# Maxima over partitions by two float32 products instead of GpSimd's all-reduce, the FFN scales placed earlier, and layer 0 waiting per channel half

## The chip, the cores and the metric

The kernel runs on one core of one Trainium2 chip. The metric is the device time of one execution in microseconds. A core has five engines with queues of their own, each worked through in order: PE (TensorE, the matrix engine), DVE (VectorE), ACT (ScalarE), POOL (GpSimd) and SP (SyncE, which issues the DMAs here). They meet only at semaphores.

## What is computed

The reference is a block with attention and a feed-forward part side by side, both fed by the same layer norm. x has 16 batches of 512 tokens and 256 channels; there are 8 heads of width 128.

```python
xn = layernorm(x)                                   # over the 256 channels
q, k, v = xn @ wq, xn @ wk, xn @ wv                 # per head; q and k rotated by position (rope)
p = softmax(q @ k.T / 128 - 1e30 * (i < j))         # causal
attn = sum over heads of (p @ v) @ wo
h = s0 * concat(xn, -xn) @ sign(k0)                 # sign: +1 where the boolean is true, else -1
h = 2 * relu(h)
h = 2 * relu(s1 * h @ sign(k1))                     # 1024 -> 1024
out = x + attn + s2 * h @ sign(k2)                  # 1024 -> 256
```

All of it is float32. k0 is 512 x 1024, k1 1024 x 1024, k2 1024 x 256, and s0, s1, s2 are scalars.

## The kernel before

**Numbers.** Every float32 operand of a product is held as two half-precision parts, high and low, and a product is taken as two or three half-precision products that add up in PSUM. The weights wq, wk, wv and wo are first divided by a power of two that is worked out on the chip from the largest absolute value in each: `largest` (L254) reduces one weight along the free axis to a column per partition on VectorE; `powers` (L259) brings two such columns together over the 128 partitions with GpSimd's partition_all_reduce, cuts them to a power of two and takes its reciprocal; `split_w` (L274) writes the high part on ScalarE and the low part on VectorE. powers(0) serves wq and wk, powers(2) serves wv and wo.

**Order.** The program is written out for all 16 x 8 = 128 heads by a planner. `Fill` (L356) takes the next of 8 PSUM banks in a ring and waits for those who read it last; its products go to TensorE's queue at once, and each adds its columns/512 to a clock (L369). What the other engines do with the result is put off with `at(delay, job)` (L343) and put down by `run_due` (L347) when the clock has come that far, or earlier when `need` (L351) asks for it. So the order of each queue is fixed when the program is written.

**Before the heads.** SyncE issues the loads of x, the scales, k0, k1, wq, wk, the tables cos and sin, k2, wv, later wo. `norm`, `norm_apply` and `first_T` normalise batch 0 and turn it by float32 transposes to xT (channels on partitions, two channel halves c = 0, 1, each with a high part from ScalarE and a low part from VectorE). `subtract_k0` and `sign_k0` build W0, `convert_k1` (GpSimd and ScalarE) W1, `convert_k2` (GpSimd) W2. `ffn_scales` (L293) works out signs and factors; `convert_k1` waits for some of them. Then `layer0(0, n)` for n = 0..7 (L632) and `layer1(0, 0)`, `powers(0)`, the first quarter of wq and wk, `layer1(0, 1)`.

**Heads.** The loop over slots g = -2..129 (L796) puts down qk(g + 2, w) for w = 0 (q) and 1 (k), scores(g + 1), values(g - 1), and between them fillers (layer0, layer1, layer2, v_proj, proj) in three groups. qk (L458) has six steps of each of its two fills: ScalarE swaps the halves (L478, L479, tile tb), VectorE multiplies by cos (straight, L485, tile ta), GpSimd multiplies tb by sin and adds (crossed, L489 and L491), ScalarE takes the high part (L497), VectorE the low part (L501). scores (L508) waits for the low parts of q and k of its head. In slot -2 this stands after the two fills of qk(0): the second quarter of wq and wk, `convert_k2`, `largest` of wv and wo, `powers(2)`, both halves of wv, and `pads` (GpSimd zeroes eight strips); layer1(0, 2) and layer1(0, 3) come behind, and layer1(0, 4) is in slot -1 ahead of scores(0). `straight`, `swap` of k and `crossed` of head 0 fall due only within layer1(0, 2).

The code as it was, with the line numbers of the profile:

Of the kernel before, what the change touches and what calls it, by code (L numbers as in the profile page):

```python
# [83 lines left out]
def block_kernel(nc, x, wq, wk, wv, wo, k0, k1, k2, s3, cosT, sinT, out):  # L84
    ctx = ExitStack()
    with ctx:
        def sb(name, shape, dt=F32):
            return ctx.enter_context(nc.sbuf_tensor(name, shape, dt))
# [33 lines left out]
        RI = sb("ri", [128, 4, 4])  # L122
        RK = sb("rk", [128, 4, 4])
        S3 = sb("s3", [128, 3])
        AM = sb("am", [128, 4])
        AR = sb("ar", [128, 4])
        P2 = sb("p2", [128, 4])
        KN = sb("kn", [128, 4])
        SG = sb("sg", [128, 8])
        SC = sb("sc", [128, 8])  # L130
        BANK = [ctx.enter_context(nc.psum_tensor(f"bank{i}", [128, 512], F32)) for i in range(8)]


# [68 lines left out]

        c = pool.put(lambda e: e.memset(ID[:], 0.0))
        m = pool.put(lambda e: e.memset(MASK[:], 0.0))
        done["half"] = pool.put(lambda e: e.memset(HALF[:], -0.5))
        pool.wait(c)
        done["ident"] = pool.put(lambda e: e.affine_select(
# [44 lines left out]


        def largest(i, n):  # L254
            dve.wait(done["w_in", n])
            done["largest", i] = dve.put(lambda e: e.tensor_reduce(AM[:, i:i + 1], stage3[n], AX.XY, ALU.max,  # L256
                                                                   apply_absolute_value=True))

        def powers(i, least):  # L259

            pool.wait(done["largest", i], done["largest", i + 1])
            a = pool.put(lambda e: e.partition_all_reduce(AR[:, i:i + 2], AM[:, i:i + 2], 128,
                                                          bass.bass_isa.ReduceOp.max))
            dve.wait(a)
            a = dve.put(lambda e: e.tensor_scalar(AR[:, i:i + 2], AR[:, i:i + 2], least, None, ALU.max))
            dve.wait(a)
            a = dve.put(lambda e: e.tensor_scalar(P2[:, i:i + 2].bitcast(I32), AR[:, i:i + 2].bitcast(I32),
                                                  0x7F800000, None, ALU.bitwise_and))
            dve.wait(a)
            a = dve.put(lambda e: e.tensor_scalar(P2[:, i:i + 2], P2[:, i:i + 2], 2.0 ** -6, None, ALU.mult))  # L270
            dve.wait(a)
            done["KN", i] = dve.put(lambda e: e.reciprocal(KN[:, i:i + 2], P2[:, i:i + 2]))

# [12 lines left out]
        def signs():  # L286

            dve.wait(done["s3"])
            a = dve.put(lambda e: e.tensor_scalar(SG[:, 0:3], S3[:], 0.0, None, ALU.is_ge))
            dve.wait(a)  # L290
            done["signs"] = dve.put(lambda e: e.tensor_scalar(SG[:, 0:3], SG[:, 0:3], 2.0, -1.0, ALU.mult, ALU.add))

        def ffn_scales():  # L293

            dve.wait(done["signs"])
            dve.put(lambda e: e.tensor_scalar(SG[:, 3:4], SG[:, 1:2], 2.0 ** -8, None, ALU.mult))
            dve.put(lambda e: e.tensor_scalar(SG[:, 4:5], SG[:, 1:2], -2.0 ** -9, None, ALU.mult))
            a = dve.put(lambda e: e.tensor_tensor(SC[:, 2:4], S3[:, 0:2], SG[:, 0:2], ALU.mult))
            done["k1_signs"] = a
            dve.wait(a)  # L300
            a = dve.put(lambda e: e.tensor_scalar(SC[:, 4:5], SC[:, 2:3], SC[:, 3:4], 64.0, ALU.mult, ALU.mult))
            dve.wait(a)
            done["ffn_scale"] = dve.put(lambda e: e.tensor_scalar(SC[:, 5:6], SC[:, 4:5], S3[:, 2:3], None, ALU.mult))

# [3 lines left out]
        def subtract_k0(half):  # L308

            dve.wait(done["k_in", 0])  # L310
            done["k0_diff", half] = dve.put(lambda e: e.tensor_tensor(
                W0[:, :, half * 512:half * 512 + 512], halves(K0S[:, 0:2048], half), halves(K0S[:, 2048:4096], half),
                ALU.subtract))
# [37 lines left out]
        def need(key):  # L351
            while key not in done:
                later.pop(0)[1]()
            return done[key]
# [275 lines left out]
                  ("vp", b, grp, t, HI), ("vp", b, grp, t, LO), scale=2.0 ** -6, free=free)  # L630

        def layer0(b, n):  # L632
            pe.wait(done["W0", n // 4], need(("xT", b, 0)), need(("xT", b, 1)))
            f = Fill(("l0", b, n))
            f.group((0, 512), [(W0[:, c, n * 128:n * 128 + 128], XT[:, b % 2, s, :, c, :])
                               for c in range(2) for s in (HI, LO)])
            f.end([("h0", b, n, LO)])
            free = [("l1", b - 1, 7)] if b else []
            split(f, H0[:, HI, n, :], H0[:, LO, n, :], ("h0", b, n, HI), ("h0", b, n, LO), relu=True, free=free)
# [125 lines left out]
        act.put(lambda e: e.activation(MV[:, 1, 0, 0:1], HALF[:, 0:1], ACT.Copy))  # L765
        norm(0)
        signs()
        subtract_k0(0)
        sign_k0(0)
        norm_apply(0)  # L770
        subtract_k0(1)
        last_load()
        ffn_scales()
        first_T()
        while later:
            later.pop(0)[1]()
# [6 lines left out]
        for n in range(8):  # L783
            layer0(0, n)
            run_due()
        layer1(0, 0)
        run_due()
        powers(0, 2.0 ** -10)
# [7 lines left out]
        for g in range(-2, G + 2):  # L796
            jobs = [job for _, job in sorted(fillers.get(g, []), key=lambda item: item[0])]
            third = [jobs[k * len(jobs) // 3:(k + 1) * len(jobs) // 3] for k in range(3)]
            if g + 2 < G:
                for w in range(2):  # L800
                    qk(g + 2, w)
                    run_due()
            if g == -2:
                split_w("q", 0, 1, 4)
                split_w("k", 1, 1, 4)
                convert_k2()
                largest(2, "v")
                largest(3, "o")
                powers(2, 2.0 ** -30)
                for p in range(2):  # L810
                    split_w("v", 2, p, 2)
                pads()
            if g == -1:
                for p in (2, 3):
                    split_w("q", 0, p, 4)
                    split_w("k", 1, p, 4)
            if g == 2:
                for p in range(2):
                    split_w("o", 3, p, 2)
                done["attn_scale"] = dve.put(lambda e: e.tensor_scalar(SC[:, 6:7], P2[:, 2:3], P2[:, 3:4], None,  # L820
                                                                       ALU.mult))
            for job in third[0]:
                job()
                run_due()
            if 0 <= g + 1 < G:
                scores(g + 1)
                run_due()
            for job in third[1]:
                job()
                run_due()  # L830
            if 0 <= g - 1 < G:
                values(g - 1)
                run_due()
            for job in third[2]:
                job()
                run_due()
            if g == -1:
                normal(1)
            if g > 3 and g % 8 == 3 and g // 8 + 1 < NB:
                normal(g // 8 + 1)  # L840
# [56 lines left out]
```

How the kernel before makes its waits and increments, by code:

```python
    def wait(self, *events):  # L61
        for sem, value in events:
            if self.seen.get(id(sem), 0) < value:
                self.seen[id(sem)] = value
                self.items.append(lambda e, s=sem, v=value: e.wait_ge(s, v))
# [1 line left out]
    def put(self, make, signal=True):  # L67
        if not signal:
            self.items.append(make)
            return None
        self.count += 1
        self.items.append(lambda e: make(e).then_inc(self.sem, 1))
        return (self.sem, self.count)
# [1 line left out]
    def dma(self, make, sem, value):  # L75
        self.items.append(lambda e: make(e).then_inc(sem, 16))
        return (sem, value)
```

## Time and profile before

| | |
|---|---|
| three runs | 1819.17, 1819.51 and 1821.78 us, median 1819.51 |
| profiled execution | 1822.18 us, its span 1820.1 us |
| mean granted TensorE clock | 0.988 |
| busy share | TensorE 97%, VectorE 79%, ScalarE 60%, GpSimd 57% |
| TensorE by 40ths of the span, in tenths | 7, 5, 8, 9, 9, 7, then 9 throughout |

The span runs from the first to the last instruction; the time of an execution is a little more. Each engine's busy time counts instructions of that engine only; TensorE's ends are modelled. A timeline row stands for one instruction or for several alike, with the idle time before it and what ended that.

### The profile page before, as it was taken

The page shows a single profiled execution, that of the slowest core. Times are in us where ns is not written, and L with a number is a line of the kernel's source. Part 1 is how long each engine was busy: PE and PEld are TensorE (multiplying, and loading weights), DVE is VectorE, ACT ScalarE, POOL GpSimd, SP SyncE. Part 2 cuts the span into 40 slices and gives each one's busy share as a digit, 9 for nine tenths or more (in the row PEclk, how much of TensorE's full clock was granted, in tenths as well). Part 3 has the DMA queues.
Part 4 walks back from the last instruction along what each step waited for, and adds up shares of the span by engine and source line. Part 5 has one row for each costly group of instructions (what it writes and reads, how often), then busy time and mean ns, then how long its engine had stood idle before and what let it go on. Part 6 is the DMA issues. An engine that isn't in the chain of part 4 may idle for free.

```text
span 1820.1 us, 30382 instructions
## 1 busy us (share of the span) xinstructions
PE 1763.6 (97%) x11272; PEld 1058.5 (58%) x11272; DVE 1441.9 (79%) x3271; ACT 1092.6 (60%) x2340; POOL 1043.6 (57%) x1065
## 2 busy tenths in 40 slices
PE   7589979999999999999999999999999999999999
PEld 3255646566565666656566565566656566565566
DVE  6689878887878878788887878878797887878865
ACT  4466555665665656566665665656566665665653
POOL 2467655565655555565565655556565565655552
PEclk9899989999999999999999999999999999999999
DMA  4033524343433333442344444334433444334333
GB/s 168 18 64 70 93 47 74 83 71 76 70 71 81 68 79 64 81 78 56 84 71 76 69 72 82 66 77 67 78 80 54 86 70 76 67 73 82 64 70 65
DMA packets 454820, 133.84 MB, mean 74 GB/s; under 512 B 434704, under 2 KB 453648, under 8 KB 454672
## 3 DMA queue, kind: packets, MB, share of 16 engines
q1 hardware_dynamic: 454672, 131.90, 38.1%
q8 instruction: 89, 1.46, 0.3%
q14 instruction: 59, 0.48, 0.1%
HBM read 14.94 MB, written 8.39 MB: 13 GB/s over the span
## 4 chain that ended last, share of the span: by engine, by line
PE 89%; DVE 6%; ACT 3%; issue 1%; POOL 1%; DMA 0%; SPq 0%; DVEq 0%; POOLq 0%
PE bank L368 89%; DVE ph L566 1%; ACT p L543 1%; DVE p L529 1%; DVE ta L485 1%; POOL ta L491 0%; DVE h L410 0%; DVE v L413 0%; DVE qk L501 0%; DMA o<-in_k 0%; DVE am L256 0%; POOL tb L489 0%; ACT tb L479 0%; DVE nm L537 0%; ACT tb L478 0%
## 5 line engine op out<-in xcount | busy, mean ns | idle before, releaser
L560 POOL TENSOR_SCALAR ph<-p,ri 128x512 f16<-128x512 f32 (+3 forms) x512 | 340.4, 665 | 312.4 <-DVE rk L550 277.6
L489 POOL TENSOR_TENSOR tb<-tb,sin 128x512 f32<-128x512 f32 x256 | 329.1, 1286 | 310.1 <-ACT tb L479 299.7
L368 PE MATMUL bank<-h,w 128*128 128x512 f16 x2048 | 462.4, 379 | 0.0
L491 POOL TENSOR_TENSOR ta<-ta,tb 128x512 f32<-128x512 f32 x256 | 344.7, 1347 | 71.7 <-DVE ta L485 55.5
L543 ACT ACTIVATE p<-p,nm,sc 128x512 f32<-128x512 f32 (+3 forms) x512 | 327.3, 641 | 39.9 <-DVE nm L537 39.9
L368 PEld LDWEIGHTS bank<-h,w 128*128 128x128 f16 x2048 | 199.0, 98 | 217.9
L478 ACT ACTIVATE tb<-bank 64x512 f32<-64x512 f32 x256 | 152.1, 594 | 286.2 <-PE bank L368 275.6
L566 DVE SCALAR_TENSOR_TENSOR ph<-p,rk,ph 128x512 f16<-128x512 f32 (+3 forms) x512 | 306.1, 638 | 3.5 <-POOL ph L560 3.5
L497 ACT ACTIVATE qk<-ta 128x512 f16<-128x512 f32 x256 | 160.1, 625 | 189.8 <-POOL ta L491 189.7
L368 PE MATMUL bank<-qk 128*128 128x512 f16 (+3 forms) x1536 | 234.1, 303 | 31.7 <-DVE qk L501 31.7
L485 DVE TENSOR_TENSOR ta<-bank,cos 128x512 f32<-128x512 f32 x256 | 175.4, 686 | 90.8 <-ACT tb L479 90.3
L529 DVE CUSTOM_DVE_ANT_0 p<-bank,mask 128x512 f32<-128x512 f32 (+3 forms) x512 | 226.4, 485 | 23.9 <-PE bank L368 23.3
L368 PE MATMUL bank<-pt,v 128*128 128x256 f16 (+1 forms) x2304 | 232.7, 256 | 2.5 <-DVE ta L485 1.6
L368 PEld LDWEIGHTS bank<-pt,v 128*128 128x128 f16 x2304 | 204.5, 98 | 49.3 <-issue 2.4
L501 DVE TENSOR_TENSOR qk<-ta,qk 128x512 f16<-128x512 f32 x256 | 215.7, 842 | 13.4 <-ACT qk L497 12.3
L368 PEld LDWEIGHTS bank<-qk 128*128 128x128 f16 x1536 | 135.1, 99 | 137.7 <-DVE qk L501 35.1
L405 ACT ACTIVATE h<-bank 128x512 f16<-128x512 f32 x256 | 148.6, 587 | 71.6 <-PE bank L368 70.1
L368 PE MATMUL bank<-xT,wq 128*128 128x512 f16 x768 | 186.7, 379 | 1.6 <-DVE h L410 1.6
L368 PE MATMUL bank<-xT,wk 128*128 128x512 f16 x768 | 186.6, 379 | 0.0
L368 PE MATMUL bank<-wv,xT 128*128 128x512 f16 x768 | 181.6, 379 | 2.2 <-DVE ta L485 2.2
L410 DVE SCALAR_TENSOR_TENSOR h<-bank,h 128x512 f16<-128x512 f32 x256 | 172.4, 684 | 8.9 <-ACT h L405 1.4
L368 PE MATMUL bank<-wo,o 128*128 128x256 f16 x1536 | 172.9, 273 | 0.0
(75 smaller groups left out, 1714.5 us busy)
## 6 DMA issues: line engine op xcount, KB each, us to landing
out<-xnat SPq DMA_DIRECT2D x32, 256.0 KB, 2.4
xnat<-in_x SPq DMA_DIRECT2D x15, 512.0 KB, 4.0
pt<-ph SPq DMA_TRANSPOSE x256, 4.3
o<-in_k SPq DMA_DIRECT2D x1, 1024.0 KB, 7.9
v<-in_wq SPq DMA_DIRECT2D x1, 1024.0 KB, 9.9
v<-in_wk SPq DMA_DIRECT2D x1, 1024.0 KB, 11.5
ph<-in_wv SPq DMA_DIRECT2D x1, 1024.0 KB, 13.4
o<-in_wo SPq DMA_DIRECT2D x1, 1024.0 KB, 10.8
```

Of the source, the lines that this page charges most:

```text
L368: self.todo.append(lambda e: e.matmul(self.ps[:, cols[0]:cols[1]], lhsT, rhs, start=start, stop=stop))
L410: done[lo_key] = dve.put(lambda e: e.scalar_tensor_tensor(lo_out, src, 0.0, hi_out, ALU.max, ALU.subtract))
L478: act.put(lambda e: e.activation(TB[0:64, r, :], f.ps[64:128, :], ACT.Copy))
L485: done["rot_a", n] = dve.put(lambda e: e.tensor_tensor(ta, f.ps[:, :], COS[:], ALU.mult))
L489: a = pool.put(lambda e: e.tensor_tensor(tb, tb, SIN[:], ALU.mult))
L491: done["rot", n] = pool.put(lambda e: e.tensor_tensor(ta, ta, tb, ALU.add))
L497: done["qk_hi", n] = act.put(lambda e: e.activation(hi, ta, ACT.Copy))
L501: done["qk_lo", n] = dve.put(lambda e: e.tensor_tensor(lo, ta, hi, ALU.subtract))
L529: done["max", g, i] = dve.put(lambda e, i=i, a=a, w=w: e.tensor_tensor_reduce(out=P[:, r, S_OFF[i]:S_OFF[i] + w], in0=f.ps[:, a:a + w], in ...
L543: done["exp", g, i] = act.put(lambda e: e.activation(v, v, ACT.Exp, bias=NM[:, g % 4, i:i + 1], scale=SC[:, 0:1], accum_out=SM[:, g % 4, i ...
L560: done["P_hi", g, i] = pool.put(lambda e: e.tensor_scalar(part(r, i, HI), v, RI[:, g % 4, i:i + 1], 4096.0, ALU.mult, ALU.mult))
L566: done["P_lo", g, i] = dve.put(lambda e: e.scalar_tensor_tensor(part(r, i, LO), v, RK[:, g % 4, i:i + 1], part(r, i, HI), ALU.mult, ALU.su ...
```

## The change

`powers` loses its GpSimd instruction. `largest` now writes its column into a 128-column strip of zeros (AM, float32, in the memory that xT of batch 1 uses later), one strip for each pair of weights, the pair in columns 0 and 1. `turn_largest` multiplies the strip by the identity on TensorE, so that row 0 and row 1 of a bank hold the maxima of the two weights, and VectorE reduces the 128 columns of the bank to one. `powers` cuts these to powers of two on VectorE, puts them on the diagonal of two columns (DG), and a second product with a matrix of ones (ONES) brings both numbers to all partitions; VectorE copies them from the bank and takes reciprocals. GpSimd zeroes AM and sets ONES at the start. turn_largest(0) stands ahead of layer1(0, 0); turn_largest(2) stands between layer1(0, 2) and layer1(0, 3), and powers(2), the split of wv and the pads stand behind layer1(0, 3).

`ffn_scales` moves from behind the second `subtract_k0` to ahead of the first. `layer0` waits for channel half 0 of xT before its first two products and for half 1 before its last two.

```diff
-        AM = sb("am", [128, 4])
+        DG = sb("dg", [128, 4])
...
+        AM = XT[:, 1].rearrange("p s t c n -> p (s t c n)").bitcast(F32)[:, 0:256].rearrange("p (i n) -> p i n", i=2)
+        ONES = XT[:, 1].rearrange("p s t c n -> p (s t c n)").bitcast(F32)[:, 256:384]
...
+        done["am_zero"] = pool.put(lambda e: e.memset(AM, 0.0))
+        done["ones"] = pool.put(lambda e: e.memset(ONES, 1.0))
...
         def largest(i, n):
-            dve.wait(done["w_in", n])
-            done["largest", i] = dve.put(lambda e: e.tensor_reduce(AM[:, i:i + 1], stage3[n], AX.XY, ALU.max,
+            dve.wait(done["w_in", n], done["am_zero"])
+            done["largest", i] = dve.put(lambda e: e.tensor_reduce(AM[:, i // 2, i % 2:i % 2 + 1], stage3[n], AX.XY, ALU.max,
                                                                    apply_absolute_value=True))
+        def turn_largest(i):
+            pe.wait(done["largest", i], done["largest", i + 1], done["am_zero"], done["ident"])
+            f = Fill(("am", i))
+            f.mm((0, 128), AM[:, i // 2], ID[:], True, True)
+            f.end([("am_max", i)])
+            dve.wait(done[f.key])
+            done["am_max", i] = dve.put(lambda e: e.tensor_reduce(AR[:, i:i + 1], f.ps[:, 0:128], AX.X, ALU.max))
         def powers(i, least):
-            pool.wait(done["largest", i], done["largest", i + 1])
-            a = pool.put(lambda e: e.partition_all_reduce(AR[:, i:i + 2], AM[:, i:i + 2], 128,
-                                                          bass.bass_isa.ReduceOp.max))
+            dve.wait(done["am_max", i])
+            a = dve.put(lambda e: e.tensor_scalar(AR[:, i:i + 1], AR[:, i:i + 1], least, None, ALU.max))
             dve.wait(a)
...
+            a = dve.put(lambda e: e.tensor_scalar(AR[:, i + 1:i + 2].bitcast(I32), AR[:, i:i + 1].bitcast(I32),
                                                   0x7F800000, None, ALU.bitwise_and))
             dve.wait(a)
-            a = dve.put(lambda e: e.tensor_scalar(P2[:, i:i + 2], P2[:, i:i + 2], 2.0 ** -6, None, ALU.mult))
+            a = dve.put(lambda e: e.tensor_scalar(DG[:, i:i + 2], ID[:, 0:2], AR[:, i + 1:i + 2], 2.0 ** -6,
+                                                  ALU.mult, ALU.mult))
+            pe.wait(a, done["ones"])
+            f = Fill(("p2", i))
+            f.mm((0, 2), ONES, DG[:, i:i + 2], True, True)
+            f.end([("KN", i)])
+            dve.wait(done[f.key])
+            a = dve.put(lambda e: e.tensor_scalar(P2[:, i:i + 2], f.ps[:, 0:2], 1.0, None, ALU.mult))
             dve.wait(a)
             done["KN", i] = dve.put(lambda e: e.reciprocal(KN[:, i:i + 2], P2[:, i:i + 2]))
...
         def layer0(b, n):
-            pe.wait(done["W0", n // 4], need(("xT", b, 0)), need(("xT", b, 1)))
+            pe.wait(done["W0", n // 4])
             f = Fill(("l0", b, n))
-            f.group((0, 512), [(W0[:, c, n * 128:n * 128 + 128], XT[:, b % 2, s, :, c, :])
-                               for c in range(2) for s in (HI, LO)])
+            for c in range(2):
+                f.wait(need(("xT", b, c)))
+                for s in (HI, LO):
+                    f.mm((0, 512), W0[:, c, n * 128:n * 128 + 128], XT[:, b % 2, s, :, c, :], c + s == 0, c + s == 2)
...
         signs()
+        ffn_scales()
         subtract_k0(0)
...
         last_load()
-        ffn_scales()
...
+        turn_largest(0)
         layer1(0, 0)
...
                 largest(3, "o")
-                powers(2, 2.0 ** -30)
-                for p in range(2):
-                    split_w("v", 2, p, 2)
-                pads()
...
+            if g == -2:
+                turn_largest(2)
             for job in third[2]:
                 job()
                 run_due()
+            if g == -2:
+                powers(2, 2.0 ** -30)
+                for p in range(2):
+                    split_w("v", 2, p, 2)
+                pads()
```

## Rows read from the trace of the kernel before

**Rows 1.** Waits of TensorE, whole span: total us, times, longest us.

```profile
PE bank L368 <- DVE qk L501: 31.7, 7, 17.2
```

**Rows 2.** Timeline of TensorE: start us, us, what, xcount, idle before.

```profile
28.87 1.46 PE L368 MATMUL bank<-xT,wq 128*128 128x512 f16 x6
...
31.46 7.07 PE L368 MATMUL bank<-h,w 128*128 128x512 f16 x32
...
40.95 3.62 PE L368 MATMUL bank<-h,w 128*128 128x512 f16 x16
61.75 3.18 PE L368 MATMUL bank<-qk 128*128 128x512 f16 x12 [17.18 <-DVE qk L501]
...
77.71 1.79 PE L368 MATMUL bank<-qk 128*128 128x512 f16 x12
```

**Rows 3.** Windows: length, busy us (x count) by engine, granted clock, DMA share, GB/s.

```profile
60.00:62.00 2.00, 0.25 (x1) 0.14 (x2) 0.98 (x2) 1.70 (x3) 0.22 (x1) 0.50 0.00 0
80.00:100.00 20.00, 16.05 (x104) 9.46 (x103) 19.89 (x44) 13.43 (x30) 13.30 (x13) 1.00 0.35 66
300.00:600.00 300.00, 300.00 (x1927) 179.81 (x1925) 241.59 (x555) 183.02 (x392) 177.09 (x179) 1.00 0.39 75
```

**Rows 4.** Timeline of VectorE from 35 to 66 us, as rows 2.

```profile
35.88 2.27 DVE L256 TENSOR_REDUCE am<-o 128x1 f32<-128x2048 f32 x1
...
43.84 2.48 DVE L283 SCALAR_TENSOR_TENSOR wv<-ph,kn,wv 128x1024 f16<-128x1024 f32 x2 [1.22 <-ACT wv L281]
...
60.91 0.69 DVE L501 TENSOR_TENSOR qk<-ta,qk 128x512 f16<-128x512 f32 x1 [0.62 <-ACT qk L497]
62.89 1.11 DVE L283 SCALAR_TENSOR_TENSOR wq<-v,kn,wq 128x512 f16<-128x512 f32 x1 [1.29 <-ACT wq L281]
...
65.92 1.28 DVE L485 TENSOR_TENSOR ta<-bank,cos 128x512 f32<-128x512 f32 x2
```

**Rows 5.** Timeline of ScalarE from 30 to 58 us, as rows 2.

```profile
30.98 0.59 ACT L479 ACTIVATE tb<-bank 64x512 f32<-64x512 f32 x1
...
42.66 2.19 ACT L281 ACTIVATE wv<-ph,kn 128x1024 f16<-128x1024 f32 x2 [9.73 <-DVE kn L272]
...
57.36 0.63 ACT L497 ACTIVATE qk<-ta 128x512 f16<-128x512 f32 x1 [11.28 <-POOL ta L491]
```

**Rows 6.** Timeline of GpSimd from 11 to 56 us, the same columns.

```profile
11.71 5.91 POOL L326 TENSOR_SCALAR w<-o,sg 128x1024 f16<-128x1024 uint8 x5 [4.88 <-DVE sc L298]
24.86 0.37 POOL L262 PARTITION_ALL_REDUCE ar<-am  x1 [7.24 <-issue]
33.10 2.43 POOL L334 TENSOR_SCALAR w<-o 128x2048 f16<-128x2048 uint8 x1 [7.86 <-issue]
41.44 0.37 POOL L262 PARTITION_ALL_REDUCE ar<-am  x1 [5.92 <-issue]
46.44 1.23 POOL L223 MEMSET ph<- 128x128 f16 x8 [4.62 <-DVE wv L283]
54.73 1.26 POOL L489 TENSOR_TENSOR tb<-tb,sin 128x512 f32<-128x512 f32 x1 [7.06 <-issue]
```

**Rows 7.** Timeline of all engines at the start, as rows 2.

```profile
7.68 1.23 DVE L311 TENSOR_TENSOR w<-o 128x1024 f16<-128x1024 uint8 x1 [1.66 <-DMA o<-in_k]
...
11.14 1.08 ACT L405 ACTIVATE xT<-bank 128x512 f16<-128x512 f32 x2 [1.05 <-PE bank L372]
...
11.81 0.21 DVE L303 TENSOR_SCALAR sc<-sc,s 128x1 f32<-128x1 f32 x1
11.94 1.28 DVE L413 SCALAR_TENSOR_TENSOR xT<-bank,xT 128x512 f16<-128x512 f32 x2
...
13.36 8.76 PE L368 MATMUL bank<-xT,w 128*128 128x512 f16 x32 [2.05 <-ACT w L319]
```

**Rows 8.** Groups by line and form: busy us, mean ns, idle before.

```profile
L529 DVE CUSTOM_DVE_ANT_0 p<-bank,mask 128x128 f32<-128x128 f32 x128 | 36.4, 285 | 0.0
L372 PE MATMUL bank<-ident,xp 128*128 128x128 f32 x8 | 1.9, 424 | 9.4 <-DVE xp L250 9.4
```

More of the change, by code:

```diff
@@ L259, in powers @@
         def powers(i, least):
-            pool.wait(done["largest", i], done["largest", i + 1])
-            a = pool.put(lambda e: e.partition_all_reduce(AR[:, i:i + 2], AM[:, i:i + 2], 128,
-                                                          bass.bass_isa.ReduceOp.max))
+            dve.wait(done["am_max", i])
+            a = dve.put(lambda e: e.tensor_scalar(AR[:, i:i + 1], AR[:, i:i + 1], least, None, ALU.max))
             dve.wait(a)
-            a = dve.put(lambda e: e.tensor_scalar(AR[:, i:i + 2], AR[:, i:i + 2], least, None, ALU.max))
@@ L266, in powers @@
-            dve.wait(a)
-            a = dve.put(lambda e: e.tensor_scalar(P2[:, i:i + 2].bitcast(I32), AR[:, i:i + 2].bitcast(I32),
+            a = dve.put(lambda e: e.tensor_scalar(AR[:, i + 1:i + 2].bitcast(I32), AR[:, i:i + 1].bitcast(I32),
                                                   0x7F800000, None, ALU.bitwise_and))
             dve.wait(a)
-            a = dve.put(lambda e: e.tensor_scalar(P2[:, i:i + 2], P2[:, i:i + 2], 2.0 ** -6, None, ALU.mult))
+            a = dve.put(lambda e: e.tensor_scalar(DG[:, i:i + 2], ID[:, 0:2], AR[:, i + 1:i + 2], 2.0 ** -6,
+                                                  ALU.mult, ALU.mult))
```

## The prediction

> **What bounds the kernel now.** I read four views, in this order. First the waits of TensorE [rows 1]: it stands 31.7 us in seven waits for line 501, and one of the seven is 17.2 us; the other six come to 14.5 us, 2.4 us each. Then its timeline [rows 2]: layer1(0, 4) begins at 40.95 and ends at 44.57, and the next product, scores(0), begins at 61.75. That hole is the largest thing in the span that is not work. From 300 us on TensorE is busy in 300.00 of 300 us at full clock [rows 3], so whatever the first 62 us give back, the rest should pass on whole.
>
> Then the hole is followed back. scores(0) waits for the low part of the rotated k of head 0, VectorE's line 501 at 60.91 [rows 4], which waits for line 497 on ScalarE, and that had waited 11.28 us for GpSimd [rows 5]. GpSimd's own timeline [rows 6] shows the reason: its first rotation product (tb, line 489) begins at 54.73 after 7.06 us idle that end on "issue", which means that nothing the profile sees was missing. Its operand, the swapped halves, was written by 31.57 (30.98 + 0.59) [rows 5]. Before that the same timeline has three more such holes: 7.24 us before the first all-reduce over partitions, 7.86 us before k2's conversion behind it, 5.92 us before the second all-reduce. I read this as 6 to 8 us for every change from ordinary work to the all-reduce or back; the five conversions at 11.71, which waited for VectorE alone, show no such hole. The second reason is order: straight(0), swap(1) and crossed(0) were put down behind powers(2), the split of wv and the pads, so line 485 for head 0 could run only after the split of wv (43.84 + 2.48 = 46.32) [rows 4], and tb only after the pads (46.44 + 1.23 = 47.67) [rows 6].
>
> Here the Trainium skill speaks against the change: GPSIMD Engine Reference, section 4.1 (Engine selection), gives reductions along the partition dimension to GpSimd. The all-reduce itself is indeed shown with 0.37 us [rows 6], less than any replacement; the four holes, 28.1 us together, are not in that figure. Section 2.1 (Instruction dispatch) of the same page has a first call to a freshly loaded kernel pay about 6 us with no instruction shown, 5.95 us in its measurement. The trace agrees with the size (5.92 to 7.86) but shows it four times for one kind of kernel, on the way back too. With 5.95 in place of 7.06 for the last hole the removed time would be 1.1 us less; my sum does not go by either, since it is built from the new order below.
>
> **The change part by part.**
>
> *FFN scales ahead of k0.* VectorE is idle 1.66 us before 7.68, until k0 lands; five operations of 0.14 to 0.21 us [rows 7] fit there: cost nothing (0.8 us if k0 came earlier). They leave the place before 11.94, where they stood until 12.02 in front of the low parts of xT. ScalarE has the first high part done at about 11.7 (11.14, two in 1.08), so the first low part runs 11.75 to 12.4 in place of 11.94 to 12.6, the second ends near 13.0. GpSimd's conversion of k1 may start up to 1.4 us earlier than 11.71; layer 1 needs it near 22 and it ended at 17.6, so nothing.
>
> *Layer 0 waits per channel half.* Its first product starts after channel 0's low part, at 12.5 in place of 13.36 [rows 7]; the two products of channel 0 (8.76/32 = 0.27 each) last about until channel 1 is there. Gain 0.8 us, between 0 and 0.9. All of it is in front of weights that come later, so by itself it moves little.
>
> *powers(0).* TensorE gets a 128x128 float32 product after layer 0 and a two-column one after layer1(0, 0). The trace has no plain float32 product. The nearest row is the float32 transpose, 0.424 us each [rows 8]; a half-precision product of as many columns is 3.62/16/4 = 0.06 us [rows 2]. Ends: 0.06 and 0.85 (twice the transpose); I take 0.42 and 0.25. On VectorE a reduction of 128 columns of PSUM comes in: nearest row 0.285 us [rows 8], ends 0.2 and 0.6, taken 0.3. It stands in VectorE's queue ahead of three low parts of layer 0 and waits for TensorE to finish layer 0 at 21.3 and the product at 21.7; the three then end at 24.0 (3 x 0.64), and layer1(0, 0), which began at 21.7, needs the last of them at 24.8. No stall. The maxima over q and k come ahead of all low parts of layer 0 in VectorE's queue, so they are ready. Then three small operations, the second product at 25.2, two small ones: the reciprocal stands near 25.9, and before it stood at 26.05 (25.23, where the all-reduce ended, and four operations of 0.2 at most [rows 7]). So wq and wk split as before, and the 0.8 us won at layer 0 is spent on the two products: qk(0) begins at 28.8 +- 0.5, as before (28.87) [rows 2].
>
> *The second turn, and what moved.* layer1(0, 2) runs 31.46 to 35.0 as before. Behind it on TensorE now stands turn_largest(2), which waits for VectorE's maximum over wo: 35.88 + 2.28 = 38.15 [rows 4]. This is the added wait: TensorE stands 3.2 us, layer1(0, 3) is queued behind it. Product 38.2 to 38.6, layer1(0, 3) to 42.1. Meanwhile the rotation of head 0 is no longer behind wv. VectorE: straight(0) 38.15 to 38.8, straight(1) to 39.4, the reduction to 39.7. GpSimd has no hole left, and tb is done at 32.8, 1.26 after the swap (k2's conversion can follow k1's, ended at 17.6, since the row names nothing that it waited for); ta 38.85 to 40.1 (1.26) [rows 6]. ScalarE 40.15 to 40.8 (0.63) [rows 5], VectorE's low part to 41.4 (0.69), a low part of layer 1 to 42.1 (0.64), three small ones to 42.7. Second product 42.7 to 42.95 (TensorE stands another 0.6), copy and reciprocal to 43.4. ScalarE splits wv to 45.6 (2.19), then turns to the high part of k of head 0, to 46.3. VectorE: wv 44.6 to 47.05, a low part of layer 1 to 47.7, line 501 for k to 48.35. TensorE: qk(1) 42.95 to 45.6 (31.46 - 28.87 = 2.6), layer1(0, 4) to 49.2. So scores(0) begins at 49.2, bound by TensorE's own work by 0.8 us: 12.55 us before 61.75.
>
> *Behind scores(0).* Before, its twelve products took 3.18 us, since the granted clock stood at 0.50 at the hole's end [rows 3], the 1.2 GHz level; at 77.71 the same twelve took 1.79 [rows 2]. With TensorE busy from 42.7 on, 1.4 us more are won: 13.95 at scores(1). The other engines' chain runs from line 501 for k (60.91 before, 47.7 new) through four splits to straight(2). Before, 65.92 - 60.91 = 5.0, of which 1.29 was a wait for ScalarE's split of wq [rows 4]; ScalarE now is ahead of VectorE: 3.7, so straight(2) at 51.4, 14.5 us earlier. In 80 to 100 us VectorE is busy 19.89 of 20 and TensorE only 16.05 [rows 3]: that stretch follows VectorE's chain, so its 14.5 counts more than TensorE's 13.95. I take 14.3. The wv split and pads end near 48.3 and are wanted only by what follows scores(0): nothing. The two new strips that GpSimd fills at the start (AM, ONES) stand in its first 3 us, before anything needs them: nothing (0.5 us if they were late).
>
> Sum: 0 (start) + 12.55 (the hole's 17.2, less 3.8 of new standing and 0.7 for the two later products, to rounding) + 1.75 (1.4 of clock, and 0.35 of VectorE's lead where TensorE follows it) = 14.3 us. The profiled execution took 1822.18 around a span of 1820.10; the runs' median is 1819.51, 2.7 below it. The gain is a difference inside the span, so it comes off the median: 1805.2.
>
> **Rivals.**
>
> *The clock falls in the new wait* (chance 0.20). TensorE stands 3.2 us at turn_largest(2); if its clock drops to 0.50 as after the hole, layer1(0, 3) loses 1.4 us and the second product comes 0.8 later. For it: a stop costs the clock here already [rows 3]. Against: 3.2 is far from 17.2. scores(0) at 50.6, the rest 0.7 late: gain 13.0, 1806.5.
>
> *GpSimd's holes stay* (0.08): they belong to first uses of code, not to the all-reduce. For it: "issue" names no cause. Against: line 334's operation ran five times as line 326 before its hole. Then k2's conversion ends as late as 35.5, tb after a hole of 7.06 at 43.9, ta 45.1, and by the same steps scores(0) comes near 54 with a fallen clock: gain 7 to 9, 1811.
>
> *Given back later* (0.04): the six other waits, 14.5 us, hang on something that does not move, and grow by what is won. Against: no load is in the chains there, each wait is for line 501. 1819, within 0.2% (3.6 us, about what a measurement can tell).
>
> *Slower by a shifted order* (0.03). The four new fills add 1.0 to the planner's clock and four places to the bank ring; jobs go down by that clock. If a tie flips so that once in a batch scores waits as it does in the six other waits, 2.4 us, 15 batches cost 36: 1841. It decides from six such waits (14.3/2.4). Against: all due times are relative to the same clock, and the steady stretch has no slack to show [rows 3].
>
> *More than forecast* (0.03): with VectorE ahead, waits between 80 and 100 (3.95 us of TensorE's 20) shrink too: 1802.
>
> **Numbers.** My forecast holds 0.62, with 1803.5 to 1807 of its own. The range 1801 to 1811 takes in the fallen clock, the larger gain, twice the float32 price on both products in the path, and the edge of the staying holes. Faster: 0.62 + 0.20 + 0.08 + 0.03 = 0.93; within 0.2% 0.04; slower 0.03.
>
> **What would show it.** No holes on "issue" in GpSimd's timeline; tb of head 0 in the thirties; TensorE idle 3 us near 35 with VectorE's line 256 as its end, and under 1 us near 42; scores(0) at 49 and quick; the wait list's 17.2 gone. Wrong if a hole stands before line 489, if a wait for line 501 over 4 us remains before 60, or if TensorE is not full after 300.

## The result and the profile after

Beside four runs of the kernel before (median 1820.06 us) the changed kernel took 1807.28 us (four runs, 1804.13 to 1809.90): ratio 0.9928, 95% interval 0.9910 to 0.9946, so 12.8 us less by the medians. Timed again later on one chip with others (e9 below) it took 1807.09 against 1818.63, ratio 0.9931 (0.9917 to 0.9946). Forecast were 1805.2 us, a gain of 14.3, in a range of 1801 to 1811. The two profiled executions of the table are at the slow end of their kernels' runs. Below, "after" is the profile of the changed kernel.

| us | before | after |
|---|---|---|
| profiled execution, its span | 1822.18, 1820.1 | 1809.90, 1808.0 |
| TensorE busy in the span | 1763.6 | 1765.8 |
| longest wait of TensorE for the rotation's low part | 17.2 | 7.5 |
| scores(0) begins | 61.75 | 50.82 |
| straight(2), head 1's first rotation product on VectorE, begins | 65.92 | 53.80 |

In the changed file the lines lie lower: products L385 (L368 before), tb and ta on GpSimd L506 and L508 (L489, L491), straight on VectorE L502 (L485), the rotation's low part L518 (L501), `split_w` on VectorE L300 (L283), `largest` L260 (its column AM lies in xT's memory, so rows call it xT).

TensorE's waits after (total us, times, longest), to be held against [rows 1]:

```profile
PE bank L385 <- DVE qk L518: 14.4, 6, 7.5
...
PE bank L385 <- DVE xT L260: 3.6, 1, 3.6
```

The 17.2 is gone and the six others are left, 14.4 us as against 14.5, the longest 7.5. The new entry is the wait of turn_largest(2) for the maximum of wo. TensorE's timeline after, against [rows 2]:

```profile
12.68 9.90 PE L385 MATMUL bank<-xT,w 128*128 128x512 f16 x32 [1.29 <-DVE xT L430]
22.42 0.39 PE L385 MATMUL bank<-ident,xT 128*128 128x128 f32 x2
22.64 3.62 PE L385 MATMUL bank<-h,w 128*128 128x512 f16 x16
26.09 0.28 PE L385 MATMUL bank<-dg,xT 128*128 128x2 f32 x2
...
29.68 1.46 PE L385 MATMUL bank<-xT,wq 128*128 128x512 f16 x6
...
39.48 0.76 PE L385 MATMUL bank<-ident,xT 128*128 128x128 f32 x2 [3.60 <-DVE xT L260]
40.04 4.76 PE L385 MATMUL bank<-h,w 128*128 128x512 f16 x16
44.63 0.28 PE L385 MATMUL bank<-dg,xT 128*128 128x2 f32 x2
...
50.82 1.79 PE L385 MATMUL bank<-qk 128*128 128x512 f16 x12
...
65.39 1.79 PE L385 MATMUL bank<-qk 128*128 128x512 f16 x12
```

A float32 product shows as two instructions. The one of 128 columns holds the next product up by 0.22 us (22.42 to 22.64), the one of two columns by 0.14. layer1(0, 3) at 40.04 takes 4.76 where such a fill takes 3.62. The windows say why (columns as in [rows 3]):

```profile
36.00:38.00 2.00, 0.00 (x0) 0.00 (x0) 2.00 (x2) 0.00 (x0) 0.00 (x0) 1.00 0.00 0
38.00:39.00 1.00, 0.00 (x0) 0.00 (x0) 1.00 (x1) 0.00 (x0) 0.00 (x0) 0.96 0.00 0
39.00:40.00 1.00, 0.52 (x2) 0.53 (x3) 1.00 (x3) 0.00 (x0) 0.00 (x0) 0.50 0.00 0
...
42.00:44.00 2.00, 2.00 (x10) 0.85 (x9) 1.89 (x4) 0.49 (x2) 1.92 (x2) 0.91 0.00 0
```

TensorE did nothing from 35.9, and its granted clock fell to 0.50, the 1.2 GHz level, near 39 and was back at full within 42 to 44. GpSimd after, against [rows 6]:

```profile
18.54 1.90 POOL L351 TENSOR_SCALAR w<-o 128x2048 f16<-128x2048 uint8 x1 [1.37 <-DMA o<-in_k]
32.47 1.27 POOL L506 TENSOR_TENSOR tb<-tb,sin 128x512 f32<-128x512 f32 x1 [12.03 <-ACT tb L496]
40.08 1.26 POOL L508 TENSOR_TENSOR ta<-ta,tb 128x512 f32<-128x512 f32 x1 [6.34 <-DVE ta L502]
```

From 11 us on no hole ends on "issue" any more: k2's conversion waits for its load, tb for its swap, ta for VectorE. VectorE after, against [rows 4]:

```profile
33.16 1.12 DVE L300 SCALAR_TENSOR_TENSOR wq<-v,kn,wq 128x512 f16<-128x512 f32 x1 [1.96 <-ACT wq L298]
...
37.07 2.27 DVE L260 TENSOR_REDUCE xT<-o 128x1 f32<-128x2048 f32 x1
39.26 1.27 DVE L502 TENSOR_TENSOR ta<-bank,cos 128x512 f32<-128x512 f32 x2
...
42.04 1.08 DVE L518 TENSOR_TENSOR qk<-ta,qk 128x512 f16<-128x512 f32 x1 [1.31 <-ACT qk L514]
...
49.53 0.68 DVE L518 TENSOR_TENSOR qk<-ta,qk 128x512 f16<-128x512 f32 x1
50.12 0.75 DVE L300 SCALAR_TENSOR_TENSOR wq<-v,kn,wq 128x512 f16<-128x512 f32 x1
50.79 1.77 DVE L300 SCALAR_TENSOR_TENSOR wk<-v,kn,wk 128x512 f16<-128x512 f32 x1
...
53.80 1.27 DVE L502 TENSOR_TENSOR ta<-bank,cos 128x512 f32<-128x512 f32 x2
```

The low part of head 0's k (L518 at 49.53) now ends before TensorE comes to scores(0), but straight(2) stands 4.27 us behind it, since one of four like splits took 1.77 in place of 0.75.

### The profile page after: what moved, and what is told of

It is laid out like the page before. It is cut to its first block, busy times and chain, and to the rows that moved or that the text cites. A ratio compares the mean times of both kernels' runs of the same rounds, so it can differ in the third digit from the quotient of the medians.

```text
span 1808.0 us, 30390 instructions
## 1 busy us (share of the span) xinstructions
PE 1765.8 (98%) x11280; PEld 1058.0 (59%) x11280; DVE 1448.0 (80%) x3275; ACT 1092.7 (60%) x2340; POOL 1041.2 (58%) x1065
## 4 chain that ended last, share of the span: by engine, by line
PE 90%; DVE 6%; ACT 3%; POOL 1%; DMA 0%; issue 0%; SPq 0%; DVEq 0%; POOLq 0%
PE bank L385 90%; DVE ph L583 1%; ACT p L560 1%; DVE p L546 1%; DVE ta L502 1%; DVE h L427 0%; DVE qk L518 0%; DVE v L430 0%; DMA o<-in_k 0%; POOL ta L508 0%; DVE xT L260 0%; DVE nm L554 0%; ACT tb L496 0%; ACT tb L495 0%; DVE wo L300 0%
## 5 line engine op out<-in xcount | busy, mean ns | idle before, releaser
L506 POOL TENSOR_TENSOR tb<-tb,sin 128x512 f32<-128x512 f32 x256 | 328.9, 1285 | 311.8 <-ACT tb L496 308.4
L385 PE MATMUL bank<-h,w 128*128 128x512 f16 x2048 | 463.9, 380 | 0.0
L508 POOL TENSOR_TENSOR ta<-ta,tb 128x512 f32<-128x512 f32 x256 | 344.8, 1347 | 77.7 <-DVE ta L502 61.6
L385 PEld LDWEIGHTS bank<-h,w 128*128 128x128 f16 x2048 | 199.1, 98 | 218.4 <-issue 1.5
L502 DVE TENSOR_TENSOR ta<-bank,cos 128x512 f32<-128x512 f32 x256 | 175.4, 686 | 90.4 <-ACT tb L496 90.4
L385 PE MATMUL bank<-qk 128*128 128x512 f16 (+3 forms) x1536 | 232.7, 302 | 14.4 <-DVE qk L518 14.4
L385 PE MATMUL bank<-pt,v 128*128 128x256 f16 (+1 forms) x2304 | 232.9, 256 | 2.5 <-DVE ta L502 1.6
L385 PEld LDWEIGHTS bank<-pt,v 128*128 128x128 f16 x2304 | 204.1, 98 | 49.8 <-issue 2.4
L518 DVE TENSOR_TENSOR qk<-ta,qk 128x512 f16<-128x512 f32 x256 | 214.5, 838 | 3.3 <-ACT qk L514 2.5
L385 PEld LDWEIGHTS bank<-qk 128*128 128x128 f16 x1536 | 134.6, 98 | 119.5 <-DVE qk L518 17.4
L385 PE MATMUL bank<-xT,wq 128*128 128x512 f16 x768 | 186.7, 379 | 1.6 <-DVE h L427 1.6
L385 PE MATMUL bank<-xT,wk 128*128 128x512 f16 x768 | 186.7, 379 | 0.0
L385 PE MATMUL bank<-wv,xT 128*128 128x512 f16 x768 | 181.6, 379 | 2.4 <-DVE ta L502 2.4
L385 PE MATMUL bank<-wo,o 128*128 128x256 f16 x1536 | 172.9, 273 | 0.0
## 6 DMA issues: line engine op xcount, KB each, us to landing
o<-in_wo SPq DMA_DIRECT2D x1, 1024.0 KB, 10.7
```

The costliest lines, as they stand in the source:

```text
L385: self.todo.append(lambda e: e.matmul(self.ps[:, cols[0]:cols[1]], lhsT, rhs, start=start, stop=stop))
L502: done["rot_a", n] = dve.put(lambda e: e.tensor_tensor(ta, f.ps[:, :], COS[:], ALU.mult))
L506: a = pool.put(lambda e: e.tensor_tensor(tb, tb, SIN[:], ALU.mult))
L508: done["rot", n] = pool.put(lambda e: e.tensor_tensor(ta, ta, tb, ALU.add))
L518: done["qk_lo", n] = dve.put(lambda e: e.tensor_tensor(lo, ta, hi, ALU.subtract))
```

## The experiments

My theory: the gain has two parts, GpSimd's holes at each change to and from the all-reduce, and the order that lets head 0's rotation go ahead of wv. The rivals: only the holes count; only the order counts.

**e1: the order without the products.** The whole change, but `powers` as before:

```diff
 # before, with the two start edits, and in slot -2:
-    powers(2, ...); split_w("v", ...) x2; pads()     # behind largest(3, "o")
+    powers(2, ...); split_w("v", ...) x2; pads()     # behind layer1(0, 3)
```

> The whole change but for the products: GpSimd's all-reduce stays, and powers(2), the split of wv and the pads stand behind layer1(0, 3). My theory (holes and order each hold a part): four holes of 6 to 8 us on GpSimd remain, but tb and ta of head 0 run ahead of the third; the third and the fourth now delay wv's split and tb of head 1; scores(0) near 55, straight(2) near 59, ta of head 1 near 64 (66.74 before), gain over the kernel before 2 to 5 us. Rival 'only the order counts': gain 12 as in the whole change. Rival 'only the holes count': gain 0.

Measured: 1818.93 against 1819.40 us, ratio 1.0001 (0.9991 to 1.0010): nothing, at most 1.6 us. GpSimd's timeline:

```profile
34.70 1.69 POOL L489 TENSOR_TENSOR tb<-tb,sin 128x512 f32<-128x512 f32 x1
...
50.28 0.37 POOL L262 PARTITION_ALL_REDUCE ar<-am  x1 [5.72 <-issue]
55.28 1.23 POOL L223 MEMSET ph<- 128x128 f16 x8 [4.63 <-DVE wv L283]
63.55 1.26 POOL L489 TENSOR_TENSOR tb<-tb,sin 128x512 f32<-128x512 f32 x1 [7.04 <-issue]
```

tb of head 0 did move ahead (54.73 before), and scores(0) began at 56.51, 5.2 us earlier. But the two holes only moved behind it: the last now stands in front of tb of head 1, whose ta follows at 64.89 as against 66.74 before. I had expected 2 to 5 us; of the 5.2 not even 2 can be seen in the time. scores(0) was not the place to measure, and straight(2), 7.0 us earlier (58.92), was not either, since the last hole stands behind both; ta of head 1 was, only 1.85 us earlier.

**e2: the products without the order.** turn_largest(2), powers(2), the split of wv and the pads directly behind `largest(3, "o")`:

```diff
 # on the changed kernel, which has these lines around layer1(0, 3)
                 largest(3, "o")
+                turn_largest(2)
+                powers(2, 2.0 ** -30); split_w("v", 2, p, 2) x2; pads()
```

> The products in place of the all-reduce, but turn_largest(2), powers(2), the split of wv and the pads directly behind the maxima of wv and wo as before the change. My theory: no holes on GpSimd; TensorE stands some 7 us behind qk(0) until the maximum of wo (39), layer 1 runs behind it with a fallen clock; scores(0) near 55, gain over the kernel before 6 to 9 us. Rival 'only the holes count': gain 12. Rival 'only the order counts': gain 0 to 2.

Measured: 1810.75 against 1819.40, ratio 0.9954 (0.9941 to 0.9967): 6.0 to 10.7 us less, as expected. TensorE:

```profile
37.46 0.76 PE L385 MATMUL bank<-ident,xT 128*128 128x128 f32 x2 [6.68 <-DVE xT L260]
39.24 0.59 PE L385 MATMUL bank<-dg,xT 128*128 128x2 f32 x2 [1.02 <-DVE dg L280]
39.70 8.85 PE L385 MATMUL bank<-h,w 128*128 128x512 f16 x32
...
54.42 1.79 PE L385 MATMUL bank<-qk 128*128 128x512 f16 x12
```

By the medians the products alone are worth 8.6 us, the order alone 0.5, both together 11.5 to 12.8: the new order pays 3 to 4 us, and only once the holes are gone. The intervals of e2 and of the whole change overlap, and against e3, timed beside e2, the medians differ by 1.9 us only; the traces show the part more clearly, with straight(2) 47.9 us behind the first transpose in e2 (56.47, 8.55) and 44.4 in the changed kernel (53.80, 9.45). "Only the order counts" falls by both runs. "Only the holes count" fits e1 (0) and falls by e2, where its 12 us lie outside the interval and a part is left for the order.

**e3 and e4: the two start edits left out, and alone.**

```diff
 # e3, on the changed kernel; e4 has the reverse on the kernel before
-        ffn_scales()                 # ahead of subtract_k0(0)
+        ffn_scales()                 # behind last_load()
-            for c in range(2): f.wait(need(("xT", b, c))) ...
+            pe.wait(done["W0", n // 4], need(("xT", b, 0)), need(("xT", b, 1))); f.group(...)
```

> The change without the two edits of the start (FFN scales back behind the second subtract_k0, layer 0 waits for both channel halves). My theory: what layer 0 wins comes in front of weights that come later, so the time is that of the whole change within 1 us (1806 to 1809); layer 0 begins near 13.4 in place of 12.7. Rival 'the start passes on': 0.7 to 0.9 us slower than the whole change.

> The kernel before with the two edits of the start alone. My theory: layer 0 begins near 12.6 in place of 13.36, the hole of 17 us before scores(0) stays as it hangs on GpSimd; gain 0 to 0.9 us, which can't be told from nothing. Rival: 1 us or more.

Measured: e3 1808.83, ratio to before 0.9942 (0.9928 to 0.9955), which overlaps the changed kernel's 0.9931 and can't be told from it; e4 1818.52, ratio 0.9996 (0.9988 to 1.0005), nothing. The moment at which k0 lands differs between executions (the first transposes begin between 8.4 and 9.9), so starts are read from there: layer 0 begins 3.23 us behind the first transpose with the edits (after, e1, e2, e4 and others alike) and 3.98 without. But its 32 products take 8.35 to 10.02 us with the edits, in most traces over 9.1, and 8.54 to 8.76 without; the products at the start stand 0.43 us apart, twice the later spacing, though the granted clock reads 1.00 there, and that stretch is mostly longer where layer 0 starts earlier; why is not shown. So in most traces what is won at its start is gone at its end (not in e4 and e12).

**e5: two all-reduces that nobody reads**, in the changed kernel:

```diff
                 convert_k2()
+                for i in range(2):   # IDLE is a new tile
+                    pool.put(lambda e, i=i: e.partition_all_reduce(IDLE[:, 2*i:2*i+2], HALF[:, 2*i:2*i+2], 128, ReduceOp.max))
```

> The changed kernel with two all-reduces over partitions behind k2's conversion that nobody reads. My theory (a hole stands at each change between ordinary work and the all-reduce): 6 to 8 us idle on 'issue' before the first, under 0.5 us before the second, 6 to 8 us before tb of head 0 (line 489 of the kernel before). GpSimd would reach tb near 35 to 36 in place of 32.5, and ta is held by VectorE until 40 anyway, so the time stays within 2 us of the changed kernel. Rival 'each all-reduce takes its 6 to 8 us': a hole before both, none before tb. Rival 'first use of code': a hole before the first, none before the second and none before tb.

GpSimd, and the swap that writes tb on ScalarE:

```profile
17.79 1.90 POOL L352 TENSOR_SCALAR w<-o 128x2048 f16<-128x2048 uint8 x1 [1.54 <-DMA o<-in_k]
25.82 0.72 POOL L829 PARTITION_ALL_REDUCE idle<-half  x2 [6.13 <-issue]
33.97 1.26 POOL L507 TENSOR_TENSOR tb<-tb,sin 128x512 f32<-128x512 f32 x1 [7.43 <-ACT tb L497]
```
```profile
30.37 0.59 ACT L497 ACTIVATE tb<-bank 64x512 f32<-64x512 f32 x1
```

One hole of 6.13 before the first, none between the two, 7.43 from their end to tb. The profile puts the last down to the swap, but that had ended at 30.96, 3.0 us before. So a hole belongs to each change, in and out, as the theory has it. "Each all-reduce takes its time" (two holes in, none out) falls. "First use of code" falls by e1 above: tb's first run there stands directly behind k2's conversion (34.70), and 7.04 us stand before a later one. (In the changed kernel tb came behind a wait of 12.03 us, which could have hidden a hole.) Two things go with this. The eight memsets behind the second all-reduce began without a hole on "issue", and the 7.06 us came behind them [rows 6]. And of the 5.92 us before that all-reduce only 3.3 held anything up, since the maximum of wo ended at 38.15 [rows 4]. The one time, 1809.17, is within the changed kernel's runs.

**e6 and e11: TensorE kept busy in the new wait.** Sixteen products that nobody reads ahead of turn_largest(2); in e11 they don't count on the planner's clock:

```diff
+                now = clock[0]                                   # e11
+                for i in range(4):
+                    f = Fill(("warm", i))
+                    for n in range(4):
+                        f.mm((0, 512), W0[:, 0, 0:128], XT[:, 0, HI, :, 0, :], n == 0, n == 3)
+                    f.end([])
+                clock[0] = now                                   # e11
                 turn_largest(2)
```

> The changed kernel with sixteen products that nobody reads (3.5 us) ahead of turn_largest(2), where TensorE stood 3.60 us and its clock fell to 0.50. If the fallen clock has a price of its own: granted clock 1.00 from 34 to 46, layer1(0, 3) takes 3.6 in place of 4.76, scores(0) 0.5 to 1.1 us earlier (near 50), straight(2) up to 0.9 us earlier. If VectorE's chain sets both anyway: layer1(0, 3) 3.6, scores(0) and straight(2) unchanged within 0.3.

> As e6, sixteen products that nobody reads ahead of turn_largest(2), but they don't count on the planner's clock, so that every queue keeps the changed kernel's order. My theory: granted clock 1.00 throughout, layer1(0, 3) 3.6 us, TensorE stands 0.9 us at the second product, straight(2) 14.3 us behind the end of the maximum of wo (14.5 in the changed kernel's profile, 16.2 in e5): the wait itself costs VectorE's chain nothing, its fallen clock 0 to 1.9 us. Rival 'the extra products cost': more than 15.

e6 did not keep the order and settles nothing: its sixteen units on the planner's clock brought line 518 of k ahead of powers(2) on VectorE, the second product waited 2.58 us for that, and scores(0) was 51.33. The clock did stay at 1.00. e11 keeps the order; TensorE and VectorE:

```profile
39.36 3.63 PE L385 MATMUL bank<-h,w 128*128 128x512 f16 x16
43.69 0.38 PE L385 MATMUL bank<-dg,xT 128*128 128x2 f32 x2 [0.71 <-DVE dg L280]
```
```profile
38.63 1.27 DVE L502 TENSOR_TENSOR ta<-bank,cos 128x512 f32<-128x512 f32 x2
...
52.96 1.27 DVE L502 TENSOR_TENSOR ta<-bank,cos 128x512 f32<-128x512 f32 x2
```

TensorE in e3, where the clock did not fall in a wait of the same length:

```profile
37.82 0.46 PE L385 MATMUL bank<-ident,xT 128*128 128x128 f32 x2 [3.60 <-DVE xT L260]
38.12 3.62 PE L385 MATMUL bank<-h,w 128*128 128x512 f16 x16
```

From straight(0) to straight(2) VectorE's chain takes 14.33 us in e11. In the changed kernel's profile it takes 14.54 (layer1(0, 3) 4.76 us), in e3 14.33 (3.62), in e5 16.17 (6.38, the clock at 0.50 until past 42). So the wait costs this chain nothing, since VectorE itself is what TensorE waits for; its fallen clock costs 0.2 us in one execution and 1.8 in another, and nothing where it does not fall. e11's one time, 1809.79, shows no gain from it.

**e12: tb of head 1 held behind VectorE's four splits.**

```diff
                 pool.wait(done["swap", n], done["sin"])
+                if n == 2: pool.wait(done["W", "k", 3])
```

> The changed kernel, but GpSimd's tb of head 1's q (the one that ran beside VectorE's four splits of wq and wk) waits until the last of the four is done. In the changed kernel one of the four took 1.77 us and the others 0.74, and tb 1.68 where it takes 1.27 alone. Theory 'the two engines stand in each other's way when VectorE reads two operands from SBUF': all four splits take 0.74 to 0.75, tb 1.27, straight(2) begins 1.0 us earlier behind line 501 of head 0's k (3.2 to 3.3 in place of 4.27), ta of head 1's q ends 0.3 to 0.7 us earlier although tb starts 2 us later. Rival 'the long split has another cause': 1.77 stays, and ta of head 1 ends 1 us later.

VectorE, then GpSimd:

```profile
47.26 0.68 DVE L520 TENSOR_TENSOR qk<-ta,qk 128x512 f16<-128x512 f32 x1
47.86 0.75 DVE L300 SCALAR_TENSOR_TENSOR wq<-v,kn,wq 128x512 f16<-128x512 f32 x1
48.52 0.75 DVE L300 SCALAR_TENSOR_TENSOR wk<-v,kn,wk 128x512 f16<-128x512 f32 x1
...
50.51 1.29 DVE L502 TENSOR_TENSOR ta<-bank,cos 128x512 f32<-128x512 f32 x2
```
```profile
50.74 1.27 POOL L508 TENSOR_TENSOR tb<-tb,sin 128x512 f32<-128x512 f32 x1 [2.65 <-DVE wk L300]
52.09 1.27 POOL L510 TENSOR_TENSOR ta<-ta,tb 128x512 f32<-128x512 f32 x1
```

All four splits take 0.75, tb 1.27 in place of 1.68, and straight(2) stands 3.25 us behind the low part in place of 4.27. ta of head 1 ends 6.10 us behind it (6.36 in the changed kernel), though tb waited 2.65. The one time, 1805.41, lies within the changed kernel's runs and shows no gain by itself.

**e7, e8 and e10: a better order.** e7 (and e10, the same kernel timed beside e9) splits the second quarter of wq and wk a slot later, so that VectorE has the maxima of wv and wo earlier; e8 also moves the last two quarters:

```diff
-                split_w("q", 0, 1, 4); split_w("k", 1, 1, 4)     # slot -2, ahead of the maxima
-            if g == -1:  for p in (2, 3): ...
+            if g == -1:  for p in (1, 2, 3): split_w("q", 0, p, 4); split_w("k", 1, p, 4)     # e7
+            # e8: p = 1 in slot -1, p = 2 and 3 in slot 0
```

> The changed kernel with the second quarter of wq and wk split a slot later, so that VectorE takes the maxima of wv and wo 3.5 us earlier. My theory: the added wait goes: the maximum of wo ends near 36, TensorE stands under 0.5 us at turn_largest(2) and up to 1.3 at the second product, clock 1.00, scores(0) at 46 to 48 (50.8), straight(2) at 50 to 51.5 (53.8), the whole 2 to 4 us less than the changed kernel (1803 to 1805). Rival 'given back later': the waits from 62 to 120 grow by what is won, time as the changed kernel.

> As e7, and the third and fourth quarters of wq and wk are split behind qk(2) in place of behind qk(1). My theory: VectorE's chain from line 501 of head 0's k to straight(2) holds two splits in place of six: straight(2) 2 to 3 us earlier than in e7 (47.5 to 49). The four splits then fall where VectorE is busier: 3 us back at most, so 0 to 3 us less than e7. Rival: they cost what they won, the time as e7 or 1 us more.

> The changed kernel, timed beside e10 on one chip. 1806 to 1809 us, 10 to 14 us under the kernel before. If its clock falls in the 3.6 us wait is open: straight(2) begins 14.3 us behind the end of the maximum of wo where it doesn't, up to 16.2 where layer1(0, 3) runs wholly at 1.2 GHz.

> The kernel of e7 beside the changed kernel on one chip. My theory: the 2.9 us by which straight(2) came earlier in e7 pass on, ratio of its median to e9's 0.997 to 0.999. Rival 'given back later': 0.9995 to 1.0005.

e7 took 1803.91, ratio to before 0.9921 (0.9907 to 0.9934). On one chip e10 took 1804.65 and the changed kernel (e9) 1807.09: 0.9987 by the medians, inside what the theory expected; the runs overlap (1804.47 to 1805.10 as against 1804.69 to 1809.90). TensorE in e7:

```profile
35.27 0.46 PE L385 MATMUL bank<-ident,xT 128*128 128x128 f32 x2
...
40.11 0.38 PE L385 MATMUL bank<-dg,xT 128*128 128x2 f32 x2 [0.93 <-DVE dg L280]
...
46.40 1.79 PE L385 MATMUL bank<-qk 128*128 128x512 f16 x12
...
70.42 2.74 PE L385 MATMUL bank<-wv,xT 128*128 128x512 f16 x6 [3.52 <-DVE ta L502]
```

The new wait is gone and scores(0) is 4.4 us earlier, straight(2) 3.1 (50.71); a part comes back at 70.42 as a longer wait for VectorE (2.38 in the changed kernel). e8 took 1804.89, no better than e7: straight(2) came at 48.72, but the moved splits fell beside tb and ta again, in VectorE's timeline of e8:

```profile
64.44 1.83 DVE L300 SCALAR_TENSOR_TENSOR wq<-v,kn,wq 128x512 f16<-128x512 f32 x1
66.19 1.75 DVE L300 SCALAR_TENSOR_TENSOR wk<-v,kn,wk 128x512 f16<-128x512 f32 x1
```

There the rival held: they cost what they won. e7 has the lowest median seen; it beats the kernel before clearly, and the changed kernel by about 0.13%, which the overlap of the runs leaves likely and not certain.

## Why the prediction was right, and where its sizes were off

The direction, the mechanism and the range were right; the time is 2.1 us above the forecast value, 0.3 above its own narrow range, and next to the rival of the fallen clock (1806.5). That nearness is luck: the clock did fall in the profiled execution, but it cost 0.2 us on the chain that counts, not the 1.3 by which that rival was priced; the rest of the loss comes from VectorE's durations, below.

- *GpSimd's holes stand at each change to and from the all-reduce*: shown by e5. The rival "each all-reduce" is refuted by the same run, "first use" by e1. The Trainium skill's GPSIMD Engine Reference, section 2.1 (Instruction dispatch), has the first call to a freshly loaded kernel pay about 6 us. By that rule e5's second all-reduce is free, and the trace agrees (6.13 us before the first, none before the second); the 7.43 us on the way back stand in the trace alone.
- *Order and holes both hold a part*: shown by e1 and e2, with the addition that the order is worth nothing by itself (at most 1.6 us), since the last hole then stands in the next rotation.
- *FFN scales and layer 0 cost and bring nothing*: right, but not for the reason given. I had layer 0 end 0.8 us earlier and the float32 products take that back. The products were cheap (0.22 and 0.14 us in TensorE's queue, forecast 0.42 and 0.25); layer 0 itself ate the lead, 9.90 us for 32 products as against 8.76 [rows 7]. So qk(0) began at 29.68, not 28.8.
- *TensorE stands 3.2 us at turn_largest(2)*: 3.60. The clock fell; I had given that 0.20 and 1.3 us. Its price on the chain that counts is 0.2 us in after, 0.5 in e12 and 1.8 in e5.
- *scores(0) at 49.2*: 50.82, a gain of 10.9 in place of 12.55 (the parts given for it, 17.2 less 3.8 and 0.7, come to 12.7).
- *The stretch behind follows VectorE's chain*: it fits here, and is not shown. straight(2) came 12.12 us earlier, the six later waits 12.1 to 12.2, and the span ended 12.1 us earlier, while scores(0) had moved by 10.9; but scores(1) had moved by 12.3 (77.71 to 65.39), too near to tell them apart. From 300 us on TensorE is full as before.
- *The six other waits*: they are not 2.4 us each, which is their mean, but 0.5 to 7.5 (7.46 at 250.01 before, 7.46 at 237.85 after). The price of the rival "slower by a shifted order" rests on that mean. None of the six grew, so "given back later" falls too.
- *straight(2) at 51.4*: the mis-sized term, 53.80. Of the 2.4 us, 1.1 had come by straight(0) (39.26, forecast 38.15): 0.8 from the late qk(0) and 0.37 from a split of 1.12 beside tb, in place of the 0.75 that it takes in e5, where tb comes later. The other 1.3 lie between straight(0) and straight(2) (14.54, forecast 13.25). Up to the low part of k it is 0.7 (10.27, forecast 9.55): 0.4 is the low part of q at 42.04, 1.08 in place of 0.69 beside GpSimd's tb and ta (1.07 in the kernel before too, at 58.02), and 0.2 the clock (10.06 in e3 and e11). From there it is 0.6 (4.27, forecast 3.7): the split of 1.77 costs 1.02, as e12 shows with 3.25, but the 3.7 was read from a stretch in which one split had already taken 1.11 beside tb [rows 4], and so held a part of that. I had taken VectorE's durations over from the old order and not asked what GpSimd would run beside them in the new one.

What stays open: why the changed kernel's runs spread over 5.8 us (1804.13 to 1809.90). The new wait is not needed for it: 23 runs of the kernel before spread over 7.2 (1815.39 to 1822.62). The traces show three parts: the landing of k0 (1.5 us), the fall of the clock in the new wait (0 to 1.8), and its fall in waits that both kernels have. Scores behind the wait of 4.0 us near 250, in after and in e7:

```profile
252.45 3.36 PE L385 MATMUL bank<-qk 128*128 128x512 f16 x12 [3.99 <-DVE qk L518]
```
```profile
248.46 1.79 PE L385 MATMUL bank<-qk 128*128 128x512 f16 x12 [4.00 <-DVE qk L518]
```

From there to the end of the span it is 1555.6 us in after and 1553.1 in e7; 1.6 of the difference are these twelve products. e10's five runs lie within 0.6 us, but those of e7, the same kernel, within 3.1, so that this order is steadier is not shown.

## What to carry to other kernels

Holes that end on "issue" on both sides of one kind of instruction can belong to its price (two of them back to back, as in e5, show it), which the 0.37 us of its row doesn't show. Where two causes stand one behind the other, as holes and order here, taking away one of them may buy nothing: follow the chain past the first hole to the next use of the same engine. And durations read while a neighbour stood idle no longer hold once a new order lets it work beside them.

## What the runs showed of the hardware

- VectorE's operations that read two tensors from SBUF and GpSimd's that read from it slow each other. VectorE's split takes 0.75 us alone and 1.12 or 1.77 beside GpSimd's tb, which itself goes from 1.27 to 1.68 (after, e12); it took 2.13 beside k2's conversion in e4 and 2.38 beside that and tb in e1. In these rows the one that began first keeps its time and the other is longer: in after the split at 50.12 takes 0.75, tb at 50.32 0.41 more than alone, the split at 50.79 1.02 more. Straight, which reads one of its tensors from PSUM, keeps its 0.64 (two in 1.27 at 53.80, beside ta at 54.62). The Trainium skill's Advanced Engine Details and Errata, GPSIMD Details, says that the Pool engine shares a read and a write interface with DVE and conflicts with its instructions with two SBUF inputs; the traces agree and add the size.
- TensorE's clock fell in a wait of 3.60 us in three executions (layer1(0, 3) took 4.76, 4.82 and 5.30 in after, e9 and e12), in one of 3.23 (e5), and did not in another of 3.60 (e3). In a wait of 4.0 near 250 us it varied too: the twelve products of scores behind it took 3.36 in before, after and e9, 2.14 to 2.28 in e3, e10 and e12, and 1.79 in e7.
- A float32 product of 128 columns delays the next by 0.22 us at full clock, less than the 0.42 that the float32 transposes of the start suggested. These stand in front of the stretch where half-precision products too stand 0.43 apart, twice the later spacing; that this is the reason is not shown.
